# Scan's state product in 32-row by 128-column tiles, two lanes side by side, from one plain copy of the solved rows

## The reference

```python
q = short_conv(x @ Wq, conv_q); k = short_conv(x @ Wk, conv_k); v = short_conv(x @ Wv, conv_v)
def step(S, inp):                       # S: per batch and head, 128 x 64
    q_t, k_t, v_t, g_t, b_t = inp
    S = S * exp(g_t)
    u = (v_t - einsum('bhk,bhkv->bhv', k_t, S)) * b_t
    S = S + einsum('bhk,bhv->bhkv', k_t, u)
    o_t = einsum('bhk,bhkv->bhv', q_t, S)
```

## Time and profile before

| | |
|---|---|
| times of three runs | 2637.47, 2638.2, 2646.84 us; median 2638.2 |
| span of the profiled execution | 2632.2 us, 93819 instructions |
| PE busy | 2266.7 us (86%) |
| PE weight loads busy | 1651.1 us (63%) |
| DVE busy | 1903.0 us (72%) |
| ACT busy | 1354.1 us (51%) |
| POOL busy | 1137.5 us (43%) |
| state product L1122 | 2048 matmuls of 128 columns, 258.8 us busy |
| spread L1352 | x256 of 32x512, 150.5 us busy |

### The profile page before, as it was taken

One profiled execution on the slowest core, in us unless ns is written; L12 is line 12 of the kernel. 1 busy time (PEld: TensorE's weight loads), 2 busy tenths in 40 slices (PEclk: granted clock), 3 DMA queues, 4 the chain that ended last, 5 costly groups with the idle time before them and its releaser, 6 DMA issues. The chain is left out here.

```text
span 2632.2 us, 93819 instructions
## 1 busy us (share of the span) xinstructions
PE 2266.7 (86%) x36541; PEld 1651.1 (63%) x36542; DVE 1903.0 (72%) x3913; ACT 1354.1 (51%) x3667; POOL 1137.5 (43%) x1143
## 2 busy tenths in 40 slices
PE   4652999999987889899888989989898888989987
PEld 4541999999963646556565655746556565655646
DVE  5664232323228888988889899888988989888894
ACT  0001444344326655656656566655656656566663
POOL 3774444444433426253342624436253342624333
PEclk9997999999988999999999999999999999999998
DMA  5574222222210010100101000010100101000010
GB/s 168 193 248 152 72 72 73 71 72 72 72 55 21 17 44 11 36 22 25 32 15 44 21 27 23 25 44 5 42 22 25 33 14 44 23 24 22 25 29 16
DMA packets 105644, 135.05 MB, mean 51 GB/s; under 512 B 39360, under 2 KB 78816, under 8 KB 105056
## 3 DMA queue, kind: packets, MB, share of 16 engines
q0 software_dynamic: 23552, 61.38, 7.5%
q1 hardware_dynamic: 62448, 40.55, 5.8%
q10 hardware_dynamic: 19312, 28.33, 3.0%
HBM read 76.18 MB, written 54.00 MB: 49 GB/s over the span
## 5 line engine op out<-in xcount | busy, mean ns | idle before, releaser
L1458 DVE SCALAR_TENSOR_TENSOR att_cv<-att_psA,att_cw,att_cv 128x508 f32<-128x508 f32 (+2 forms) x660 | 479.2, 737 | 7.6
L1789 POOL TENSOR_TENSOR att_Sd<-att_S,att_mst 128x1024 f32<-128x1024 f32 x128 | 242.9, 1903 | 505.1 <-DVE att_S L1572 482.0
L999 PE MATMUL att_psA<-att_xt,att_wqkv 128*128 128x512 f32 x880 | 425.3, 616 | 17.0 <-DMA att_xt<-xn_cols 12.6
L1122 PE MATMUL att_psS<-att_W,att_ktok 128*128 128x128 f32 x2048 | 258.8, 280 | 12.1 <-DVE att_S L1572 6.4
L999 PEld LDWEIGHTS att_psA<-att_xt,att_wqkv 128*128 128x128 f32 x880 | 156.7, 193 | 178.7 <-issue 159.5
L734 PE MATMUL moe_psHT<-moe_xT,moe_w1s 128*128 128x128 f32 x2176 | 267.5, 276 | 0.0
L1122 PEld LDWEIGHTS att_psS<-att_W,att_ktok 128*128 128x128 f32 x2048 | 242.5, 193 | 32.9 <-issue 17.2
L675 ACT ACTIVATE moe_hT<-moe_psHT,moe_b1T 128x128 f32<-128x128 f32 x544 | 155.1, 368 | 201.1 <-PE moe_psHT L734 201.1
L744 PE MATMUL moe_psY<-moe_w,moe_hT 128*128 x1088 | 257.2, 379 | 0.0
L734 PEld LDWEIGHTS moe_psHT<-moe_xT,moe_w1s 128*128 128x128 f32 x2176 | 256.1, 193 | 0.2
L701 DVE TENSOR_TENSOR moe_y<-moe_psY,moe_b2b 128x256 f32<-128x256 f32 x136 | 57.8, 425 | 271.1 <-PE moe_psY L744 271.1
(11 more groups left out here) (247 smaller groups left out, 4382.1 us busy)
## 6 DMA issues: line engine op xcount, KB each, us to landing
expert_out<-moe_y POOLq DMA_DIRECT2D x136, 128.0 KB, 2.0
route_x_in<-in_L_attn_x_dram SPq DMA_DIRECT2D x64, 128.0 KB
xn_rows<-route_xn ACTq DMA_DIRECT2D x16, 512.0 KB, 3.6
xn_cols<-route_xnT ACTq DMA_DIRECT2D x16, 512.0 KB, 3.8
moe_w<-in_L_ffn_W_dram ACTq DMA_DIRECT2D x2, 4096.0 KB, 24.5
att_xt<-xn_cols SPq DMA_DIRECT2D x16, 512.0 KB, 4.4
att_xr<-in_L_attn_x_dram SPq DMA_DIRECT2D x64, 128.0 KB, 2.7
out_dram<-att_xr SPq DMA_DIRECT2D x256, 32.0 KB, 1.7
```

The source lines that it names most:

```text
L999: last = MM(pair_bank(m, j)[:, h, :], wqkv[:, c, (2 * j + h) * P:(2 * j + h + 1) * P], xt[:, c, :], start=(c == 0), stop=(c == DC - 1))
L1122: last = MM(pS[:, h // 4, 2 * DV * (h % 4):2 * DV * (h % 4) + 2 * DV], ktok[:, c % 2, h, :], W[:, h, 2 * two:2 * two + 2, :], start=True, ...
L1458: last = V.scalar_tensor_tensor(out=late, in0=by_lane(pair_bank(m, j)[:, h, :])[:, :, 0:LT - d], scalar=cw[:, 2 * j + h, TAPS - 1 - d:TAPS ...
L1789: G.tensor_tensor(new, old, bc(mst[:, par, c, 4 + 2 * two:6 + 2 * two, :], 3, DV), op=ALU.mult).then_inc(s["sd_done" if two else "sd_half" ...
```

## The change

The state product is made per lane instead of per pair of lanes. For lane l it takes the lane's own 32 rows of the keys and of the solved rows, on the tile of the array that starts at row 32l and is 32 rows by 128 columns; its two lanes go to different banks of `pS`. `W` no longer has blocks and zeros: it is [128, 512], a plain copy of `pC` bank 0, made by one ACT instruction (`solved`, in place of the four of `spread`). `apply_scores` reads the same copy. DVE's addition reads `pS` in the order in which `S` lies. The two memsets of `W` go, and the count of constants falls from 10 to 8. Lines after the edit of PE shift by 2 and more: L1122 becomes L1125, L1352 becomes L1350.

```diff
-        R = sb("R", [P, HV]); W = sb("W", [P, H, LANES, DV])
+        R = sb("R", [P, HV]); W = sb("W", [P, HV])
...
             def apply_state(m, c, two):
...
-                wait(pe, "w_spread", 2 * n + two + 1)
+                wait(pe, "w_copied", n + 1)
...
                 for h in range(H):
-                    last = MM(pS[:, h // 4, 2 * DV * (h % 4):2 * DV * (h % 4) + 2 * DV], ktok[:, c % 2, h, :], W[:, h, 2 * two:2 * two + 2, :],
-                              start=True, stop=True)
+                    v = slice(DV * h, DV * h + DV)
+                    for l in (2 * two, 2 * two + 1):
+                        r = lane_rows(l)
+                        last = MM(pS[:, l % 2, v], ktok[r, c % 2, h, :], W[r, v], start=True, stop=True, tile_position=(CT * l, 0))
                 last.then_inc(s["sup_ready"], 1)
...
-                wait(pe, "w_spread", 2 * n + 2)
+                wait(pe, "w_copied", n + 1)
...
-                        last = MM(pC[r, 0, DV * h:DV * h + DV], AT[r, par, c * H + h, :], W[r, h, l, :],
+                        last = MM(pC[r, 0, DV * h:DV * h + DV], AT[r, par, c * H + h, :], W[r, DV * h:DV * h + DV],
...
-            def spread(m, c):
+            def solved(m, c):
...
                 wait(act, "w_ready", n + 1)
-                for two in range(2):
-                    wait(act, "sup_ready", 2 * n - 1 + two)
-                    if two == 0:
-                        wait(act, "aw_ready", n)
-                    for l in (2 * two, 2 * two + 1):
-                        r = lane_rows(l)
-                        last = A(W[r, :, l, :], heads(pC[r, 0, :]), ACT.Copy)
-                    last.then_inc(s["w_spread"], 1)
+                wait(act, "sup_ready", 2 * n)
+                wait(act, "aw_ready", n)
+                A(W[:, :], pC[:, 0, :], ACT.Copy).then_inc(s["w_copied"], 1)
...
-                new, old = (t[:, 2 * two:2 * two + 2, :].rearrange("p l (h v) -> p h l v", h=H) for t in (S, Sd))
-                V.tensor_tensor(new, pS[:, :, :].rearrange("p b (h l v) -> p (b h) l v", l=2, v=DV), old,
-                                op=ALU.add).then_inc(s["s_done" if two else "s_half"], 1)
+                pair = slice(2 * two, 2 * two + 2)
+                V.tensor_tensor(S[:, pair, :], pS[:, :, :], Sd[:, pair, :], op=ALU.add).then_inc(s["s_done" if two else "s_half"], 1)
...
-            G.memset(W[:, 0:4, :, :], 0.0).then_inc(consts, 1)
-            G.memset(W[:, 4:8, :, :], 0.0).then_inc(consts, 1)
```

More of the change, by code:

```diff
@@ L801, in attention @@
                       "ks_ready s_read w_ready aw_ready sup_ready otr_ready wo_ready",
-            "scalar": "tap3_done tails_done silu_done sq_ready gate_done dec_done ktok_done w_spread t2_done oT_done vr_done",
+            "scalar": "tap3_done tails_done silu_done sq_ready gate_done dec_done ktok_done w_copied t2_done oT_done vr_done",
             "vector": "tap taps_done norm_read nq_done nk_done kk_used qk_used elim "
@@ L814, in attention @@
         masks = ctx.enter_context(nc.semaphore("att_masks"))
-        NCONST = 10
+        NCONST = 8
         ALONE = 20
@@ L1416, in scan @@
                         tap3_head(f, c, 0)
-                    spread(m, c)
+                    solved(m, c)
                     if c in (1, 2):
@@ L1724, in _ @@
             G.memset(sel[:, :], 0.0).then_inc(consts, 1)
-            G.memset(W[:, 0:4, :, :], 0.0).then_inc(consts, 1)
-            G.memset(W[:, 4:8, :, :], 0.0).then_inc(consts, 1)
-            G.wait_ge(consts, 8)
+            G.wait_ge(consts, 6)
             G.memset(sel[:, 32:33], 1.0).then_inc(consts, 1)
```

## The result

The changed kernel takes **2669.9 us** (median of 4 runs, 2665.7 to 2675.6), the kernel before, measured beside it, 2640.7 (4 runs, 2637.5 to 2646.8). The ratio is 1.011, 95% interval 1.008 to 1.013: slower by 29 us where +14 was forecast. The time lies in the range, the size is off. The profiled execution took 2675.6, the slowest of its four, with a span of 2673.6: 41 more than the span before. That compares two extremes. So first where these 41 lie, then how much of them belongs to every run.

A forecast was written before the change was run, and what follows sets the result against it. The prediction took PE's own queue in the scan chunks as the bound: form changes +18, ACT's copy -6.5, instruction stream +3, sum +14.5 on a 2632.2 span, plus 6.0 from span to run median: 2652 us, range 2618 to 2700.

The forecast's parts named there:

- The product: State product at L1125: 16 rounds of two lanes, each as long as one 128-column load (0.111 us), 2.02 us against 2.05.
- Rival 1: At L1125, 128-column loads of two lanes cannot run at once: round 0.222 us, 227 us more, 2879 us; chance 0.10.
- rival 2: At L1125, a 32-row load is not the bound: round 0.055 to 0.06 us, 64 us saved, 2588 us; chance 0.07.
- The edges: Changes of tile form around the state product on PE: 1.20 us per group with the product's -0.03, +18 us in all.
- whatever the change adds to PE's queue or takes from it counts in full: Scan chunks: nothing waits in PE's queue, so added or saved PE time counts fully, 4 chunks times 16 groups.
- ACT's copy: One copy of W (0.60 us) replaces four (2.40 us); only PE's waits for W at c = 3 shrink, -6.5 us.
- The instruction stream: PE's stops for issue: 16 loads and 16 matmuls more per `apply_state`, 5.6% of 52.3 us, +3 us; bounds 0 and +10.
- Rival 3: Shorter matmuls with gaps let PE's granted clock fall in the scan: at 0.9, 80 us more, 2732 us; chance 0.04.
- its own range: Range of the forecast without rivals, 2630 to 2685: form changes half as dear -9, float32 passes not alternating 10, stream +7.

## Why the prediction was right or wrong

**The product: right.** Forecast 2.02 us for 32 matmuls with rounds of one 128-column load, measured 2.00. Three kernels show the load as the price: doubling the columns doesn't lengthen the product, halving them on the whole array hardly shortens the scan, and loads of one lane in line cost 1.39 us more. The Trainium skill (TensorE: Matmul & The Clock Gate, LDWEIGHTS and Packing small matmuls) states both halves of this, that a load's time goes by its columns, and that the loads and matmuls of tiles in different row groups overlap; the trace agrees with both (193 ns at 32 and at 128 rows; 3.39 us lane by lane against 2.00). **Rival 1 and rival 2: excluded** by the same 2.00 us.

**The edges: the sizes right, the sum too large.** End to end, before and after:

```
after L999 or the decays (c = 0)         1.78 -> 1.93   +0.15 (forecast +0.16)
after L1071                              1.82 -> 1.93   +0.11 (+0.14)
between other forms                      1.98 -> 1.93   -0.05 (-0.03)
product to L999                          1.72 -> 1.91   +0.19 (+0.19)
product to the transposes (c = 3)        0.44 -> 0.59   +0.15 (+0.15)
```

Per group these give 0.49 + 0.25 + 0.25 + 0.09 = 1.08 (at c = 3 the second product waits for DVE before and after, and doesn't change), and less W's wait of 0.35 a scan should have grown by 0.73. It grew by 0.37. The step that failed is "whatever the change adds to PE's queue or takes from it counts in full". Next to the earlier trace rows there was a wait that the forecast had not read. The weight loads of the next chunk's L1082, in the kernel before and then in the changed one:

```profile
1925.60 0.49 PEld L1082 LDWEIGHTS att_psC<-att_S,att_kT 128*32 128x32 f32 x32 [0.36 <-DVE att_S L1572]
```

```profile
2284.63 0.94 PEld L1082 LDWEIGHTS att_psC<-att_S,att_kT 128*32 128x32 f32 x64 [0.17 <-issue]
```

Before, L1082 began 0.19 us later than its neighbours allowed, because DVE's addition of the state ended only then; L1145 ends in the earlier trace rows at 1925.48, and behind it L1082 would start at 1925.41 and starts at 1925.60. In the changed kernel the exit to L999 takes 0.19 us more, the addition is done by then, and the wait is gone. So the 0.19 that `L999` lost was given back a microsecond or two later, twice per group: 1.08 - 0.35 - 0.38 = 0.35, and 0.37 was measured. Over the whole attention the loads of L1082 wait for the addition 45 times before and 18 times after, 27 fewer in 15 groups. At full clock the forecast's 1.05 per scan (1.20 - 0.35 + 0.20 for the stream) was so nearly three times too large: 0.12 in the edges, 0.38 in the wait behind them, 0.20 in the stream.

**ACT's copy: right.** Forecast -6.5; PE's wait for W went from 5.7 to 0.7 us, once, in the last group, as said. With the tiles kept and the four copies back, the waits for W return (6.2 us), and the time rises by some 9 us, which the intervals don't tell apart from 6.5.

**The instruction stream: too dear.** Forecast +3, the waits for issue did not rise (87.6 and 87.5 us). The instruction queue carried 269 packets instead of 254 with no effect that can be seen.

**The clock: the term that was missing.** Rival 3 had a chance of 0.04 and a full form (0.9 in every scan, +80). It came true in part: 0.89 to 0.95 in five of the 15 scans, 22 us in the profiled execution. The argument against it was that L1082 to L1105, tiles with 64 columns too, run at full clock. Those groups were there before, between products of 128 rows; the row said nothing on a scan in which the products have few rows as well. That is the second step that failed, and it outweighs the first: the sum has +14.5 without a clock term, the scans at full clock show 5.6 (15 x 0.37), and their clock adds 22.

In the runs the clock's part is less sharp. The change has 1.008 to 1.011, the kernels with the longer stream and with 64 rows have 1.007 and 1.006; the difference, some 0.3%, is of the size of the intervals, which overlap. The granted clocks beside the same kernel before don't: 0.957 to 0.961 and 0.964 to 0.973 on the first chip. Nor are 1.007 and 1.006 the forecast's sum confirmed, though 16 to 18 us look like its 14.5. Those scans grew by just 10 and 11 us, and the clock of both kernels' runs is on average 0.005 lower than before; in their traces that lies outside the 15 scans. Why it is lower there, no run shows.

The time fell into the range partly by luck. One error made the forecast too large, another too small. The terms named for its own range reach from 2643 (-9) to 2669 (+10 and +7), not from 2630 to 2685; 2669.9 lies at their upper end, and what took it there is none of them.

What the chip reacts to is bounded, not settled. In the 15 scans neither the short stream alone nor the 32 rows alone lowered the clock, both together did, with one tile at a time more than with two, and idle time of PE was not the reason. Whether it is the rows, the columns, or their product that counts, and why nine scans of the same instructions kept full clock in one trace and six in the other, stays open.

## What to carry to other kernels

Price a product of few rows by the width of its weight load: in this kernel a 128-column load sets a step of 0.111 us, whether 32, 64 or 128 rows stand under it and whether 64 or 128 columns are streamed. So don't cut the stream, fill the round: two 64-row tiles side by side took four lanes for the price of two. Count 0.11 to 0.19 us for each edge between tile forms, look behind the edge for a wait that swallows it, and read the granted clock of the changed stretch beside its busy time before putting its length down to instructions.

## What was not expected of the hardware

- TensorE's granted clock fell to the half level in stretches where the engine was busy 96 to 100% of the time, with products of 32-row tiles and 64 columns: down to 0.89 and 0.88 over single scans with two tiles side by side, 0.69 to 0.80 with one tile at a time. The drops came out of stretches at 2.4 GHz, and nine of 15 scans of the same instructions stayed there in one trace, six in the other.
- The second lane's tiles began while the first lane's were still running, even lane by lane: its first matmul started at 1886.82 us, the first lane's last at 1887.15. So 32 pairs took 3.39 us and not 31 x 0.111 + 0.35 = 3.8.
- Whole array matmuls of 64 columns took 1.89 to 2.06 us for 16, those of 128 columns 1.95 to 2.05: a float32 pair costs its load, and the stream nothing up to there.
